# Local attention in layer 1: units of two head pairs, alternating partition halves, exponents read from PSUM, division on GpSimd

## What is computed

```python
def local_attention(q, k, v):               # 8 heads of 64, windows of 64
    bq = q.reshape(b, h, w, WINDOW, d) * QK_SCALE        # QK_SCALE = 8
    bk, bv = look_around(bk), look_around(bv)            # this window and the one before
    sim = einsum('bhwid,bhwjd->bhwij', bq, bk)
    mask = (i < j) | (i > j + WINDOW) | (j == -1)
    sim = where(mask, -max, sim)
    return einsum('bhwij,bhwjd->bhwid', softmax(sim), bv)
def _layer(x, ...):
    h = shift_token(x); q, k, v = split(h @ wqkv, 3)
    q = l2norm(q) * qs; k = l2norm(k) * ksc
    q, k = rotary_xpos(q, k)
    x = x + local_attention(q, k, v) @ wo
    ... # layernorm, gated ffn of width 341
for l in range(2): x = _layer(x, ...)       # DEPTH = 2
...
s = _L1_attn_ref(xn, ...)                   # two "time mix" layers with a scan
g = silu(_L1_ffn_ref(xn, ...))
x = x + s * g
```

## Time and profile before

| | us |
|---|---|
| median of 3 runs | 5828.37 (5816.56 to 5832.93) |
| span of the profiled execution | 5822.4 |

### The profile page before, as it was taken

The page is one execution under the profiler, slowest core; times in us unless marked ns, Lnnn a source line. Parts: engine busy times, 40 slices in busy tenths (PEclk is TensorE's granted clock), DMA queues, the critical chain, the costliest instruction groups (busy, mean ns, idle before and its releaser), DMA issues. The chain is left out here.

```text
span 5822.4 us, 60164 instructions
## 1 busy us (share of the span) xinstructions
PE 4385.6 (75%) x16724; PEld 2482.1 (43%) x16724; DVE 4514.1 (78%) x8572; ACT 2924.5 (50%) x5085; POOL 2325.4 (40%) x1980
## 2 busy tenths in 40 slices
PE   5876778767787677876778767787678866788776
PEld 1533435344353443534435344353444524444344
DVE  3678966789657996579965799658995489955898
ACT  3544645446444564445644456444564445645455
POOL 0134631447204562045620456104661046610565
PEclk9998889978899888998889988998889998899888
DMA  2000000000000000000000000000000000000000
GB/s 99 1 1 2 1 3 1 1 2 1 3 1 0 2 1 3 1 1 2 1 3 1 2 1 1 3 1 2 1 1 3 1 2 1 1 3 1 2 1 2
DMA packets 3537, 22.97 MB, mean 4 GB/s; under 512 B 336, under 2 KB 336, under 8 KB 2640
## 3 DMA queue, kind: packets, MB, share of 16 engines
q1 hardware_dynamic: 3152, 18.59, 0.8%
HBM read 16.23 MB, written 2.36 MB: 3 GB/s over the span
## 5 line engine op out<-in xcount | busy, mean ns | idle before, releaser
L1622 POOL TENSOR_SCALAR l_pp<-l_sc,l_m 128x512 f32<-128x512 f32 x496 | 783.4, 1579 | 644.3 <-DVE l_m L1572 596.7
L1572 DVE MAX8 l_m<-l_wk 128x8 f32<-128x512 f32 x1536 | 980.6, 680 | 0.0
L224 PE MATMUL bank<-l_v,l_pt 128*128 128x99 f32 (+1 forms) x5888 | 871.4, 300 | 139.5 <-ACT l_pt L1362 114.7
L224 PEld LDWEIGHTS bank<-l_v,l_pt 128*128 128x128 f32 x5888 | 814.9, 216 | 196.7 <-ACT l_pt L1362 154.0
L1316 PE MATMUL bank<-consts,l_pp 128*128 128x128 f32 x2048 | 390.9, 323 | 526.3 <-POOL l_pp L1629 519.8
L1180 POOL TENSOR_TENSOR l_hc<-l_h,l_cn 128x1024 f32<-128x1024 f32 x128 | 302.3, 2362 | 989.0 <-DVE l_h L1130 989.0
L1316 PEld LDWEIGHTS bank<-consts,l_pp 128*128 128x128 f32 x2048 | 280.2, 165 | 959.7 <-POOL l_pp L1629 828.2
L224 PE MATMUL bank<-l_km,hold 128*128 128x512 f32 x1024 | 652.7, 727 | 43.3 <-DVE l_ol L1539 18.1
L1568 DVE MATCH_REPLACE8 l_wk<-l_m,l_wk 128x512 f32<-128x512 f32 x1024 | 684.1, 675 | 0.0
L1392 ACT ACTIVATE l_sc<-bank 128x512 f32<-128x512 f32 x512 | 303.3, 594 | 739.9 <-PE bank L224 738.5
L1629 POOL TENSOR_TENSOR l_pp<-l_pp,l_ex 128x512 f32<-128x512 f32 x496 | 631.0, 1272 | 26.4 <-ACT l_ex L1399 5.7
(11 more groups left out here) (350 smaller groups left out, 8065.6 us busy)
## 6 DMA issues: line engine op xcount, KB each, us to landing
weights<-weights_dram SPq DMA_DIRECT2D x1, 11014.0 KB, 29.0
hold<-x_dram SPq DMA_DIRECT2D x9, 256.0 KB, 2.6
out_dram<-x SPq DMA_DIRECT2D x9, 256.0 KB, 3.4
consts<-consts_dram SPq DMA_DIRECT2D x1, 1503.0 KB, 32.2
rotary<-consts_dram SPq DMA_DIRECT2D x1, 1024.0 KB, 34.1
```

The lines of the kernel that those rows point to most:

```text
L224: return nc.tensor.matmul(o, lhsT, rhs, start=start, stop=stop)
L1572: nc.vector.max(m8[n % RM][:, k + 1], wk_[n % 2][:]).then_inc(S["top"], 1)
L1622: nc.gpsimd.tensor_scalar(pp[n % 2][:], sc[n % RS][:], m8[n % RM][:, 3, 0:1], None, ALU.is_ge).then_inc(S["kept"], 1)
```

## The change

All of it lies in layer 1 and its constants.

- A unit is now `u = 2 q + f`: token block q and two head pairs (g = 2f, 2f+1), both partition halves e. The score products alternate between partitions 0 to 63 and 64 to 127, into bank 2f and bank 2f+1.
- The band mask is added by PE: one bf16 product of `band` with the identity `eye` opens each of the two banks, and the scores are added onto it.
- q is no longer multiplied by its root. POOL's sum goes to `l_qk` directly (n < 4); the sums of squares of q go to 32 columns with tokens on partitions (`norms`: 4 products a block, each with 2 moving columns), and one `Ln` and one `Exp` over 32 columns make `qrs`.
- DVE takes the maximum, negated, right from the two banks (one instruction), and a tiny product forms `shift`. ACT's `exponent` is four instructions, each reading 192 (or 128) columns of PSUM with `qrs` as scale, `shift` as bias and the row sum as a second output (`zs`).
- DVE forms the reciprocal of the sums (`share`), POOL multiplies the probabilities by it, in two instructions a unit, and PE's transposes wait for that.
- The value products have `l_v` as the stationary operand (64 columns) and `l_pt` as the moving one (128 columns); they write alternately to partitions 0 to 63 and 64 to 127 of one bank, and the result already has channels on partitions. `outputs`, `turn_outputs` and the column of ones are gone; `l_of` is copied from the products' bank.
- PE's order is now: scores of u+2, transposes of u, value products of u. ACT's is: exponents of u+1, copies of u.

```diff
 def score(i, u):
-    q, e = u // 2, u % 2
+    q, f = u // 2, u % 2
     if u >= 2:
-        pe.wait_ge(S["scored"], 2 * (k - 1))
-    for f in range(2):
-        for s in range(2):
+        pe.wait_ge(S["exp"], 2 * (k - 1))
+    halves = [bank[2 * f + e].rearrange("p (s j) -> p s j", s=2)[:, :, n0:KW] for e in range(2)]
+    for e in range(2):
+        mm(halves[e], eye[:], band[:, None, n0:KW].to_broadcast([128, 2, KW - n0]), True, False)
+    for s in range(2):
+        for e in range(2):
             g = 2 * f + s
-            r = mm(bank[2 * e + f][:, 256 * s + n0:256 * s + KW],
+            r = mm(halves[e][:, s], qk[64 * e:64 * e + 64, g * T + 128 * q:g * T + 128 * q + 128],
-        r.then_inc(S["score"], 1)
+    r.then_inc(S["score"], 1)
 def attend(i, u):
-    pe.wait_ge(S["exp"], k + 1)
+    if u + 2 < NU:
+        score(i, u + 2)
+    for e in range(2):
+        if k:
+            pe.wait_ge(S["pt"], 2 * (k - 1) + e + 1)
+        pe.wait_ge(S["shared"], 2 * k + e + 1)
         ... # transposes, as before
-    if u + 2 < NU:
-        score(i, u + 2)
+    pe.wait_ge(S["pt"], 2 * k + 2)
+    for s in range(2):
+        for d in parts:
+            for e in range(2):
+                g = 2 * f + s
+                r = mm(bank[6 + q % 2][64 * e:64 * e + 64, 128 * g:128 * g + 128],
+                       vt[:, q - 1 + d, 2 * g + e], pt[e][:, 2 * s + d], d == parts[0], d == 1)
+    r.then_inc(S["pv"], 1)
-def turn_outputs(i, q):
...
 def exponent(u):
-    act(pe_[e][:, :, n0:256], pe_[e][:, :, n0:256], ACT.Exp).then_inc(S["exp"], 1)
+    a.wait_ge(S["shift"], k + 1)
+    if k >= 2:
+        a.wait_ge(S["turned"], 2 * (k - 1))
+        a.wait_ge(S["rec"], 2 * (k - 1))
+    for e in range(2):
+        for s in range(2):
+            j = 2 * e + s
+            r = act(pe_[f][:, j, WIN + n0:256], bank[2 * f + e][:, 256 * s + n0:256 * s + KW],
+                    ACT.Exp, scale=qrs[:, 2 * f + s, q, e:e + 1], bias=shift[f][:, j:j + 1],
+                    accum_out=zs[f][:, j:j + 1])
+        r.then_inc(S["exp"], 1)
...
+for u in range(NU):                       # GpSimd
+    for f in range(2):
+        g.wait_ge(S["rec"], 2 * k + f + 1)
+        nc.gpsimd.tensor_tensor(p, p, rec[e][:, 2 * f:2 * f + 2, None].to_broadcast(...),
+                                ALU.mult).then_inc(S["shared"], 1)
```

More of the change, by code:

```diff
@@ L198, in build @@
         c_sb = sb("consts", [128, once])
-        bank = [ctx.enter_context(nc.psum_tensor(f"bank{i}", [128, 512], F32)) for i in range(8)]
+        banks = ctx.enter_context(nc.psum_tensor("bank", [128, 8, 512], F32))
+        bank = [banks[:, i] for i in range(8)]
         x = sb("x", [128, T])
@@ L540, in turn_outputs @@
[L540 to L546 removed]
+                            if f == 0 and q >= 2:
+                                pe.wait_ge(S["of"], NT * i + q - 1)
@@ L669, in root @@
                             def root(n):
-                                k = 8 * i + n
-                                a.wait_ge(S["ss"], k + 1)
+                                k = 4 * i + n - 4
+                                if n < 3:
+                                    return
+                                a.wait_ge(S["ss"], 8 * i + n + 1)
+                                if n == 3:
+                                    flat = qrs[:].rearrange("p g q e -> p (g q e)")
+                                    if i:
+                                        a.wait_ge(S["shift"], NU * i)
+                                    act(flat, bank[4][:, 0:32], ACT.Ln, scale=NORM_SCALE, bias=C("floor")).then_inc(S["q_ln"], 1)
+                                    a.wait_ge(S["q_ln"], i + 1)
+                                    act(flat, flat, ACT.Exp, scale=-0.5, bias=C("norm_back")).then_inc(S["q_rs"], 1)
+                                    return
                                 if k >= 2:
@@ new lines, in share @@
+                            def share(u):
+                                f, k = u % 2, NU * i + u
+                                for e in range(2):
+                                    v.wait_ge(S["exp"], 2 * k + e + 1)
+                                    if k >= 2:
+                                        v.wait_ge(S["shared"], 2 * (k - 2) + e + 1)
+                                    nc.vector.reciprocal(rec[f][:, 2 * e:2 * e + 2], zs[f][:, 2 * e:2 * e + 2]).then_inc(S["rec"], 1)
+                            v.wait_ge(S["q_rs"], i + 1)
@@ L835, in _ @@
                             for u in range(NU):
+                                share(u)
                                 if u + 2 < NU:
                                     centre(u + 2)
-                                outputs(u)
                             v.wait_ge(S["attn"], i + 1)
```

165 lines of the change are left out of this document (75 added, 90 removed).

## The result

The changed kernel takes 5719.44 us (median of 4 runs, 5717.35 to 5724.54); the kernel before took 5822.47 us in the same set (4 runs, 5814.82 to 5832.93). The ratio is 0.9827, 95% interval 0.9812 to 0.9841: 1.7% faster. The profiled execution spans 5717.5 us against 5822.4, 104.9 less, at a mean granted clock of 0.893 against 0.895.

The account below looks back on a forecast made before the run. PE was taken to set the pace. Per pass 3.1 - 4.0 - 3.3 - 1.2 + 1.0 = -4.4 us, times 16 -70: span 5822.4 to 5752, median 6.0 above, 5758 us; range 5726 to 5860.

Parts of the forecast that it names:

- the middle: Transposes of unit 2 to those of unit 6: 16.2 us against 20.2, -4.0 a pass, with units of 4.4 us.
- start and clock: First scores to transposes of unit 2: +3.1 us a pass; +1.0 (0 to +4) for lower clock while PE waits.
- the projection: Stretch ahead of the attention loop: -1.2 us a pass (0 to -3.2), from less ACT and DVE work on q.
- 5 slots for 8 records and 9 for 16: Opposite halves overlap in a unit's scores (0.94 us against 1.50) and value products (1.05 against 1.87).
- 0.9 us of PE idle are bought: In each unit PE idles 0.9 us between transposes and value products, a wait that scores filled before.
- The two waits named: In the projection, PE's waits of 0.64 and 0.81 us for steps behind ACT's and DVE's removed work on q.
- "even" for the norms: In the projection, PE's new norms of q, 0.94 us, cost the same as half of the old 1.98 us.
- End: Transposes of unit 6 to the residual: 10.6 us against 13.9, -3.3 a pass.
- ACT, POOL and DVE keep up: In a 4.4 us unit: ACT 3.5 us (bound 4.2), POOL 1.9 (bound 2.5), DVE under 2.
- Serial halves: Rival: scores and value products of opposite halves run one after the other, +4.6 us a pass, 5902 us; chance 0.12.
- The low clock in the loop: Rival: a third of seven units at 1.2 GHz, +3.6 us a pass, 5886 us; chance 0.12.
- the forecast's own signs of being wrong: Opposite halves' records 0.1 us or more apart throughout, PE waiting for `l_shared`, or middle stretch's clock below 1.00.

Follow-up runs that it names:

- whole_array: Changed kernel with score products on all 128 rows and value products on all 128 columns, so no two run side by side; 5835.1 us.
- scores_mid: Changed kernel with the scores of unit u+2 moved between the transposes and the value products of unit u; 5834.9 us.
- roots_back: Changed kernel with ACT again running the removed Ln and Exp for the four q blocks, on data nobody reads; 5723.2 us.
- ser_scores: Changed kernel with a unit's four score products written half by half instead of alternating; 5719.8 us.
- ser_products: Changed kernel with the value products written half by half, eight records and then eight, instead of alternating; 5757.8 us.
- no_division: Changed kernel without POOL's multiplications and DVE's wait for them, transposes waiting for the exponents alone; 5721.5 us.

## Why the forecast was right in direction and too small

The mechanisms were the forecast ones, and three terms of the sum were mis-sized: the middle (-0.7 us a pass), start and clock (-0.55) and the projection (-0.45).

**Middle, -4.69 for -4.0.** The step that failed is the number of slots. I let the second record of a product go beside the first of the next, 5 slots for 8 records and 9 for 16. Records of opposite halves start together from the first, 4 and 8 slots: 0.85 us for 0.94 in the scores, 1.02 for 1.05 in the products. Masks came at 0.43 for 0.5, and the further changes of form, for which I had added 0.1, are inside these numbers. 1.83 us from the transposes to the products held to the hundredth. The unit is 4.13 for 4.4. By the terms as written, the masks and that 0.1 erred by 0.17 and the slots by only 0.12; but the slot of 0.19 held a cost of the form that comes only once in a group. At the measured 0.162 and 0.109 a slot, the two slots that I had too many are the whole 0.27. By the Trainium skill, page "TensorEngine Tiling (Array Packing)", section "Key Properties", tiles load and multiply in parallel; the trace agrees, with pairs 6 or 7 ns apart. The section's warning, that a change of the tiling mode drains the engine, fits the trace too, which shows the time though not the draining: scores are 4 slots of 0.162, 0.65 us, and 0.2 more that `whole_array`, which never changes its form, does not pay. The kernel before paid it too (8 x 0.162 + 0.2 = 1.50), so it was in my slot of 0.19 without my seeing it.

**The wait that was bought.** "0.9 us of PE idle are bought" was right as a price: the row has 0.74. It was wrong as a fate. Scores can't fill that wait (`scores_mid`) in this order of DVE's queue, but the masks can, since they wait for nothing that is young: 0.43 a unit.

**Start and clock, +3.54 for +4.1.** Here I counted the low clock twice. The row of before from which I took the third value block, "2.1 us later as before", was one in which the value projections ran at 1.2 GHz (3.35 us for four records); and I then added +1.0 for more of it. The waits ahead of the transposes of unit 0 before had a low clock too, in 11 of 16 passes, which cost up to 1.6 us each and 1.0 in the mean of all sixteen; one pass of before was not its mean. In the changed kernel, timeline of PE and ACT:

```profile
867.56 1.98 PE L227 MATMUL bank<-weights,l_hs 128*128 128x512 f32 x4
...
868.73 0.60 ACT L700 ACTIVATE l_v<-bank 128x512 f32<-128x512 f32 x1 [3.06 <-PE bank L227]
869.22 0.45 ACT L720 ACTIVATE l_probs<-bank,l_shift,l_qrs 128x128 f32<-128x128 f32 x1
...
871.14 0.50 PE L227 MATMUL bank<-band,eye 128*128 128x384 bf16 x2 [1.59 <-ACT l_probs L720]
...
872.42 0.66 PE L525 MATMUL bank<-consts,l_probs 128*128 128x128 f32 x4
```

The four records take 1.98 us, the block is copied by 3.7 us after the first masks, where I had 4.6, and the transposes of unit 0 come 6.8 us after them for 8.1. The order of the chain was as forecast: value copy, four exponents, masks and scores of unit 2, transposes. From there to unit 2 it took 6.53 for 6.3. The low clock came on top in 7 passes, 21.5 us in all or 1.3 a pass; against the 1.0 a pass of before it is hardly an addition, where I had put in 16 us for one.

**Projection, -1.65 for -1.2.** The two waits named were the right ones and went from 1.45 to 0.24 us, which is the 1.2. The stretch is 2.15 shorter at depth 0 and 1.15 at depth 1; what I had no term for is PE's wait ahead of the first scores, which went from 1.82 to 1.18 at depth 0 and from 1.61 to 2.00 at depth 1. `roots_back` gives the cause: ACT's pairs, and DVE's four multiplications for nothing that could be measured beside them. PE's own work there is 28.21 us in 30.14 for 28.27 in 31.50 (a stretch that ends in the wait, 0.7 us ahead of the first scores): "even" for the norms was right.

**End, -3.42 for -3.3.** Right.

**ACT, POOL and DVE keep up.** Exponents of 192 columns are 0.49 apart (0.52 was forecast) and POOL's products 0.83 us for 384 columns (0.95). Groups by line and shape (busy us, mean ns, idle before), which answer to the earlier trace rows:

```profile
L720 ACT ACTIVATE l_probs<-bank,l_shift,l_qrs 128x192 f32<-128x192 f32 x384 | 192.7, 530 | 1.9 <-DVE l_shift L832 1.9
...
L893 POOL TENSOR_TENSOR l_probs<-l_probs,l_rec 128x384 f32<-128x384 f32 x192 | 155.4, 827 | 203.6 <-DVE l_rec L842 203.6
...
L720 ACT ACTIVATION_READ_ACCUMULATOR l_probs<-bank,l_shift,l_qrs 128x1 f32 x512 | 114.8, 224 | 0.0
```

ACT hardly ever waits for the inputs of these exponents (1.9 us in all). The row sums' read-outs are rows of their own, but lie between the exponents without widening them, as the rows of layer 3 had suggested.

**The rivals.** Serial halves fell with the first row of PE; `whole_array` bounds what they would have given: 5835 us (without the changes of form) instead of the 5902 worked out. The unit there is 5.29, where the rival stood on 4.4 + 0.56 + 0.82 = 5.78; 0.49 for seven units and sixteen passes are 55 of the 67 us. The low clock in the loop exists, but in 5 of 16 passes of this trace and early in them; the rival put a third of all units there. One of the forecast's own signs of being wrong did appear in these five: the clock of the middle stretch averages 0.98, and the stretch is 0.2 to 0.3 us longer, because the low level lasts into it.

**The sum.** Per pass, 0.7 in the middle, 0.55 in start and clock, 0.45 in the projection and 0.1 at the end make 1.8, 29 us over 16 passes; 5.5 more came from parts that the change does not touch. Another 4 are in the 6.0 us that turned the span into a median: that set the median of several executions against the span of one, and after the change the median lies 1.9 above the span. All four terms erred to the same side, and that is what the low end did not allow for. It rested on projection and masks alone, and treated 5 and 9 slots as settled, though four slots were as open as five. It was also added up wrong: "projection at its bound and masks at theirs make 2 us more", but the projection's bound (-3.2 for -1.2) makes 2.0 by itself, and masks at 0.1 instead of 0.5 in eight units up to 3.2 more. That is up to 83 us, a low end of 5675, and 5719 would have been inside.

## What to carry to other kernels

A product that fills half of the array is worth pairing with one on the other half, in another bank or other partitions: it was worth 116 us here, and it works at the grain of records, so strict alternation isn't needed as long as blocks stay within four records. Before filling an engine's wait with more work, ask what the work waits for and who stands behind its consumer in the next queue: scores in that wait cost the whole gain, masks won 39 us. And when a stretch of one pass supplies a term, look first at the granted clock of that stretch in several passes; otherwise the low clock goes in twice, or an edit's 25 us hide behind it. An edit that is meant to change how often the clock falls needs several traces of both kernels; here there is one of each.

## What the runs showed of the hardware

- Two-pass f32 products on opposite halves start 6 or 7 ns apart and cost half: 0.162 us a pair with 192 moving columns, 0.109 with 128.
- Records of the other half start ahead of three records written before them, and were not seen ahead of more: 13 ns behind the partner where blocks are of four (`ser_scores`), 12 slots instead of 8 where they are of eight (`ser_products`).
- Going from full-array records to half-array ones and back costs about 0.1 us at each of three steps: 256, 260 and 253 ns between starts where `whole_array` has 162.
- An `Exp` of 192 columns from PSUM with scale and bias from memory and a row sum takes 530 ns, one every 490.
- The low clock comes in different passes from one execution to the next: around units 0 and 1 in five of 16 passes of the changed kernel, in one each of `ser_scores` and `no_division`, whose undisturbed passes are as long. Two kernels that differ by 25 us in their passes (`roots_back`) came out 4 us apart because of it.
